# Norm 1 made ahead of its step: statistics two steps earlier, the normalize one step earlier, the transposes of y at the head

## The reference

```python
h = tok(...)                                    # h0, (16, 256, 256)
x = layernorm(h)                                # first norm, then the layer's own norm 1
y = layer_norm(x, norm1_g, norm1_b)
q, k, v = split(y @ qkv_w.T)                    # 16 heads of 16
q, k = elu(q) + 1, elu(k) + 1
att = (q @ (k.T @ v)) / (q @ sum(k) + eps)
x = x + att @ proj_w.T + proj_b
x = x + gelu(layer_norm(x) @ fc1_w.T + fc1_b) @ fc2_w.T + fc2_b
h = h + x
h = h + (leaf_probs(sigmoid(layernorm(h) @ Wq.T @ routers.T)) @ leaf_values) @ Wout_w.T + Wout_b
```

## Time and profile before

| | us |
|---|---|
| median of 3 runs | 540.69 |
| lowest, highest | 537.18, 541.02 |
| profiled execution, its time | 536.7 |
| profiled execution, its span | 534.8 |
| PE busy | 442.4 (83%) |
| VectorE, ScalarE, GpSimd busy | 366.6, 292.2, 193.8 |
| mean granted clock of PE | 0.971 |

### The profile page before, as it was taken

How to read it: one execution, slowest core, us unless ns; L and a number is a source line. 1 busy time by engine, 2 the same in 40 slices (tenths; PEclk the granted TensorE clock), 3 DMA queues, 4 the chain that set the end, 5 groups by cost and what they waited for, 6 DMA issues and landing times.

```text
span 534.8 us, 11443 instructions
## 1 busy us (share of the span) xinstructions
PE 442.4 (83%) x3808; PEld 403.4 (75%) x3808; DVE 366.6 (69%) x867; ACT 292.2 (55%) x604; POOL 193.8 (36%) x187
## 2 busy tenths in 40 slices
PE   0076654988758998799999999999999999998983
PEld 0066654876647888688898898998998998988973
DVE  5999989996657776543747658657567566575674
ACT  3815543757566574465635744754564465366540
POOL 0597996342122212151440620810712514406110
PEclk9997997899899999999999999999999999999997
DMA  4624673425312320010100200201102001001001
GB/s 119 209 86 110 162 202 84 107 83 147 97 53 66 92 96 21 21 39 1 41 2 0 79 0 0 78 0 41 37 0 78 0 0 39 0 0 40 2 16 64
DMA packets 39872, 30.95 MB, mean 58 GB/s; under 512 B 19489, under 2 KB 35233, under 8 KB 39841
## 3 DMA queue, kind: packets, MB, share of 16 engines
q1 hardware_dynamic: 29280, 27.81, 17.2%
q10 hardware_dynamic: 10560, 2.75, 2.3%
HBM read 17.97 MB, written 12.58 MB: 57 GB/s over the span
## 4 chain that ended last, share of the span: by engine, by line
PE 54%; DVE 10%; ACT 3%; issue 3%; POOL 1%; DVEq 0%; POOLq 0%; ACTq 0%
PE PS L307 15%; PE PS L309 15%; PE PS L308 15%; PE PS L1457 5%; PE PS L1568 3%; DVE lTl L1203 1%; DVE xh L1070 1%; PE PS L1466 1%; DVE outb L1263 1%; PE PS L1499 1%; DVE bst L1209 1%; ACT lTh L795 1%; DVE x L1224 0%; DVE fc1l L1169 0%; DVE gl L1232 0%
## 5 line engine op out<-in xcount | busy, mean ns | idle before, releaser
L1232 DVE TENSOR_TENSOR gl<-PS,gh 128x512 fp32r<-128x512 f32 x56 | 38.7, 691 | 62.8 <-ACT gh L803 35.0
L800 ACT ACTIVATE PS<-PS,fc1bias 128x512 f32<-128x512 f32 x56 | 36.7, 655 | 75.3 <-PE PS L309 74.4
L307 PE MATMUL PS<-fc2h,gh 128*128 128x256 f32 x256 | 73.7, 288 | 2.9 <-DVE gl L1232 1.5
L309 PE MATMUL PS<-fc2l,gh 128*128 128x256 f32 x256 | 71.5, 279 | 0.0
L308 PE MATMUL PS<-fc2h,gl 128*128 128x256 f32 x256 | 71.4, 279 | 0.0
L529 POOL TENSOR_SCALAR pst<-mv 128x4 f32<-128x4 f32 x15 | 3.6, 243 | 179.4 <-DVE pst L1216 179.4
L307 PE MATMUL PS<-x2Th,fc1h 128*128 (+2 forms) x144 | 54.6, 379 | 1.5 <-DVE kvm L1108 1.5
L307 PEld LDWEIGHTS PS<-fc2h,gh 128*128 128x128 f32 x256 | 48.0, 188 | 7.0 <-DVE pst L1216 1.6
L308 PE MATMUL PS<-x2Th,fc1l 128*128 (+2 forms) x144 | 53.0, 368 | 0.0
L309 PE MATMUL PS<-x2Tl,fc1h 128*128 (+2 forms) x144 | 52.9, 367 | 0.0
L308 PEld LDWEIGHTS PS<-fc2h,gl 128*128 128x128 f32 x256 | 48.2, 188 | 1.0
(11 more groups left out here) (232 smaller groups left out, 1457.3 us busy)
## 6 DMA issues: line engine op xcount, KB each, us to landing
h<-h_scratch SPq DMA_DIRECT2D x16, 256.0 KB, 3.5
q_scratch<-qe SPq DMA_DIRECT2D x16, 256.0 KB, 2.4
qf<-q_scratch SPq DMA_DIRECT2D x16, 256.0 KB, 3.0
out_tokens<-outb SPq DMA_DIRECT2D x16, 256.0 KB, 2.3
h_scratch<-tokev ACTq DMA_DIRECT2D x10, 256.0 KB, 3.2
craw<-in_c_ri SPq DMA_DIRECT2D x16, 128.0 KB, 2.6
craw<-in_c_ri SPq DMA_DIRECT2D x32, 64.0 KB, 2.4
h_scratch<-tokev SPq DMA_DIRECT2D x6, 256.0 KB, 2.8
```

The costliest lines, as they stand in the source:

```text
L307: pe.matmul(dst, ah, bh, start=start, stop=False, **kw)
L309: return pe.matmul(dst, ah, bl, start=False, stop=stop, **kw)
L800: act.activation(bank(j % 2), bank(j % 2), ACT.Gelu, bias=fc1bias[:, j:j + 1]).then_inc(gact, 1)
L1232: dve.tensor_tensor(gl[:, j % 2, :], bank(j % 2), gh[:, j % 2, :].bitcast(F32), ALU.subtract).then_inc(gldone, 1)
```

## The change

The statistics get a place for each of the 16 steps, so that the wait for the other steps' use goes. stats(s+4) is made in step s while s + 4 < 8, and later by the table STATS (steps 8 and 9 at the end of step 5 and in step 6, two in step 7, then four ahead). xh(s+2) is made in step s, behind y_low(s+1) and q_elu(s) (and, from step 9 on, the mask of the first image), where xh(s+1) stood at the head of the step. T(s+1) goes to the head of step s on PE, before q(s). ScalarE does y_high(s+1) before q_parts(s). GpSimd scales earlier and waits once for xh(0) before it rotates chunk 12. One more load of h0 is issued ahead. In the loop over chunks ScalarE evacuates and stores chunk n before it makes the operands of chunk n+2.

```diff
+STATS = {5: (8,), 6: (9,), 7: (10, 11), 8: (12,), 9: (13,), 10: (14,), 11: (15,)}
...
-        bst1 = sb("bst1", [P, 2, 2, 6])
-        mv1 = sb("mv1", [P, 2, 2, 2])
-        pst1 = sb("pst1", [P, 2, 4, 2])
+        bst1 = sb("bst1", [P, STEPS, 2, 6])
+        mv1 = sb("mv1", [P, STEPS, 2, 2])
+        pst1 = sb("pst1", [P, STEPS, 4, 2])
...
# SyncE
-            load_h0(0)
-            load_h0(1)
-            load_h0(2)
+            for s in range(4):
+                load_h0(s)
...
-                load_h0(n - SINGLE + 2)
+                if n - SINGLE + 3 < GROUPS:
+                    load_h0(n - SINGLE + 3)
...
# GpSimd
-            for n in range(SINGLE, CHUNKS):
-                if n + 1 < CHUNKS:
-                    rotate((n + 1) // 2, (n + 1) % 2)
-                scales(n - FIRST + 2)
+            rotate(SINGLE // 2, 1)
+            scales(0)
+            pool.wait_ge(xh1, CREDIT + 4)
+            rotate(FIRST // 2, 0)
+            scales(1)
+            scales(2)
+            for n in range(FIRST, CHUNKS - 1):
+                rotate((n + 1) // 2, (n + 1) % 2)
+                scales(n - FIRST + 3)
...
# ScalarE, loop over chunks
+            def next_opened(it, par):
+                paired_tables(it + 1, par)
+                closed(it, par)
+                paired_operands(it + 1, par)
+                m_unshifted(it + 1, par)
...
-                    opened(it + 1, par)
-                    closed(it, par)
+                    next_opened(it, par)
...
# ScalarE, chunks 11 to 15, and a step
                 token_row(n - 1)
+                y_high(s + 1)
+                if s >= 0:
+                    q_parts(s)
                 if n + 1 < CHUNKS:
                     operands(n + 1)
-                if s >= 0:
-                    q_parts(s)
-                y_high(s + 1)
-                if n + 1 < CHUNKS:
                     tables(n + 1)
...
             def step(s):
-                q_parts(s)
                 if s + 1 < STEPS:
                     y_high(s + 1)
+                q_parts(s)
                 kv_parts(s, 0)
                 kv_parts(s, 1)
...
# VectorE
+            products(SINGLE, 7)
+            product_sums(SINGLE, SINGLE % 2)
+            norm1_stats(0)
+            one = ones[:, 0:1].unsqueeze(1)
+            link(dve.tensor_copy(vt[:, :, :, P], one.to_broadcast([P, 2, KD])))
+            link(dve.tensor_copy(vt0[:, :, :, P], one.to_broadcast([P, B, KD])))
+            dve.wait_ge(act_set, 1)
+            tt(qkvl[:, :, :], qkvraw[:, :, :], qkvh[:, :, :].bitcast(F32), ALU.subtract)
+            dve.wait_ge(ld_const, 16 * 6)
+            dve.wait_ge(b1copied, 1)
+            tt(fc1bias[:, :], fc1bias[:, :], b1add[:, :], ALU.add)
+            assert count[0] == DVE_ALL
+            norm1_apply(0)
+            norm1_stats(1)
+            products(SINGLE + 1, 7)
+            product_sums(SINGLE + 1, 1)
+            norm1_stats(2)
+            y_low(0)
+            norm1_stats(3)
+            norm1_apply(1)
+            for n in range(FIRST, CHUNKS):
                 s = n - FIRST
-                if s + 1 >= 0:
-                    norm1_apply(s + 1)
                 products(n, 7)
-                if s >= 0:
-                    q_elu(s)
                 product_sums(n, n % 2)
...
+                y_low(s + 1)
+                q_elu(s)
+                norm1_apply(s + 2)
+                if s + 4 < GROUPS:
+                    norm1_stats(s + 4)
+                k_elu(s, 0)
+                k_elu(s, 1)
 
             def step(s):
                 if s + 1 < STEPS:
-                    norm1_apply(s + 1)
+                    y_low(s + 1)
                 q_elu(s)
                 if s > GROUPS:
                     kv_mask(image(s - 1, 0))
-                if s + 1 < STEPS:
-                    y_low(s + 1)
+                if s + 2 < STEPS:
+                    norm1_apply(s + 2)
                 k_elu(s, 0)
-                if s + 2 < STEPS:
-                    norm1_stats(s + 2)
                 if s > GROUPS:
                     kv_mask(image(s - 1, 1))
+                if s > 5:
+                    for x in STATS.get(s, ()):
+                        norm1_stats(x)
                 k_elu(s, 1)
+                if s == 5:
+                    norm1_stats(STATS[5][0])
...
# PE
             def step(s):
+                if s + 1 < STEPS:
+                    y_transposes(s + 1)
                 q_products(s)
                 if s > GROUPS:
                     kv_sums(image(s - 1, 0))
-                if s + 1 < STEPS:
-                    y_transposes(s + 1)
                 kv_products(s, 0)
```

More of the change, by code:

```diff
@@ L490, in scales @@
                 pool.wait_ge(st1, CREDIT + 4 * (s + 1))
-                pool.wait_ge(xh1, CREDIT + 4 * (s - 1))
-                v = mv1[:, s % 2, :, 1]
-                pst = pst1[:, s % 2, :, :]
+                v = mv1[:, s, :, 1]
+                pst = pst1[:, s, :, :]
                 pool.tensor_scalar(pst[:, 0, :], v, EPS, None, ALU.add).then_inc(r1done, 1)
@@ L741, in _ @@
                 for par in range(2):
-                    opened(it + 1, par)
-                    closed(it, par)
+                    next_opened(it, par)
             tables(SINGLE)
+            closed(SINGLE // 2 - 1, 0)
             operands(SINGLE)
-            closed(SINGLE // 2 - 1, 0)
+            closed(SINGLE // 2 - 1, 1)
             operands(SINGLE + 1)
-            closed(SINGLE // 2 - 1, 1)
             tables(SINGLE + 1)
@@ L1056, in norm1_stats @@
                 dve.wait_ge(h0ld[s], 16)
-                dve.wait_ge(xh1, CREDIT + 4 * (s - 1))
                 for i in range(2):
-                    dve.bn_stats(bst1[:, s % 2, i, :], tile(s, i)).then_inc(st1, 1)
+                    dve.bn_stats(bst1[:, s, i, :], tile(s, i)).then_inc(st1, 1)
                 dve.wait_ge(st1, CREDIT + 4 * s + 2)
                 for i in range(2):
-                    dve.bn_aggr(mv1[:, s % 2, i, :], bst1[:, s % 2, i, :]).then_inc(st1, 1)
+                    dve.bn_aggr(mv1[:, s, i, :], bst1[:, s, i, :]).then_inc(st1, 1)
             def norm1_apply(s):
@@ L1069, in norm1_apply @@
                 for i in range(2):
-                    dve.tensor_scalar(xh[:, s % 2 * 2 + i, :], tile(s, i), mv1[:, s % 2, i, 0:1],
-                                      pst1[:, s % 2, 3, i:i + 1], ALU.subtract, ALU.mult).then_inc(xh1, 1)
+                    dve.tensor_scalar(xh[:, s % 2 * 2 + i, :], tile(s, i), mv1[:, s, i, 0:1],
+                                      pst1[:, s, 3, i:i + 1], ALU.subtract, ALU.mult).then_inc(xh1, 1)
                 m, r = (mr[:, x, s // GROUPS, image(s, 0):image(s, 0) + 2] for x in range(2))
-                r1 = pst1[:, s % 2, 2, :]
-                dve.scalar_tensor_tensor(m, mv1[:, s % 2, :, 0], -1.0, r1, ALU.mult, ALU.mult).then_inc(xh1, 1)
+                r1 = pst1[:, s, 2, :]
+                dve.scalar_tensor_tensor(m, mv1[:, s, :, 0], -1.0, r1, ALU.mult, ALU.mult).then_inc(xh1, 1)
                 dve.tensor_copy(r, r1).then_inc(xh1, 1)
@@ L1112, in _ @@
+            for n in range(FIRST, CHUNKS):
                 s = n - FIRST
-                if s + 1 >= 0:
-                    norm1_apply(s + 1)
                 products(n, 7)
-                if s >= 0:
-                    q_elu(s)
                 product_sums(n, n % 2)
-                norm1_stats(s + 2)
[L1120 to L1131, removed]
-                    y_low(s + 1)
-                if s >= 0:
-                    k_elu(s, 0)
-                    k_elu(s, 1)
+                y_low(s + 1)
@@ L1532, in _ @@
                     pe.wait_ge(dve_set, DVE_ALL)
-                if s >= 0:
-                    q_products(s)
                 if s + 1 >= 0:
@@ L1537, in _ @@
                 if s >= 0:
+                    q_products(s)
                     kv_products(s, 0)
```

## The result

The change makes the kernel faster: 519.16 us median (519.01 to 521.34) beside 539.09 (537.18 to 541.02) for the kernel before on the same chip, ratio 0.964 with a 95% interval of 0.9588 to 0.9691. The forecast was 521 in a range of 514.5 to 530; the sum of its terms, 17.0 us off the profiled execution of before (536.7), gave 519.7. The profiled execution of after took 519.01, its span is 517.2.

A forecast was written before the change was run, and what follows sets the result against it. PE was taken to wait 24.6 us for xh and the small operation behind it. Terms 3.8 + 5.3 + 10.7 - 2.8 = 17.0 us off 536.7 gave 519.7; predicted 521, range 514.5 to 530.

The forecast's parts named there:

- Head: Up to T(1), the transposes of step 1: earlier xh brings them at 90.2 us, 3.8 us less.
- Chunk steps: T(1) to T(5): steps of 6.8 us without waits for xh or GpSimd's scale, 5.3 us less.
- rotate: Rival, chunk steps: xh lands on GpSimd's rotate in all four, 9.2 us back, 530 us; chance 0.07.
- Power: Rival, chunk steps: xh waits for the GpSimd scale's power, 3.6 us in all, 525 us; chance 0.10.
- delay of up to 1 us: Chunk steps: one delay of xh by GpSimd's power, taken as absorbed by VectorE's slack.
- Plain steps: T(5) to T(10): 29.1 us in place of 39.8, 10.7 us less.
- The loop over ScalarE: Plain steps: a loop of engines through ScalarE sets each step at 4.95 us, with weight copies paid in full.
- My price of step 8: Plain steps: step 8 waits for VectorE, whose step 7 has two stats; 5.85 us.
- Late steps: T(10) to the end of kv(14,1): late mask stalls the second image's sums 0.7 us a step; 2.8 us more.
- slower: Rival, late steps: the late mask decides; 3.5 us in each of six steps eats all 17; chance 0.04.

The follow-up runs named there:

- e1: The change with xh again one step later and PE and ScalarE in their order of before; 532.52 us, ratio 0.9894 to the kernel before.
- e4: The change without GpSimd's wait for xh(0) before it rotates chunk 12; 521.79 us, ratio 0.9704 to the kernel before.
- e2: The change with the transposes behind q and ScalarE's q_parts before y_high again, xh still early; 537.81 us, ratio 0.9998 to the kernel before.
- e7: The change with one stats to a step from step 5 on; 520.1 us, ratio 0.9662 to the kernel before.
- e3: The change with VectorE's mask of the first image ahead of y_low and q_elu in the late steps; 513.42 us, ratio 0.9553 to the kernel before.
- e5: The change with only ScalarE back in its old order, q_parts before y_high; 545.9 us, ratio 1.0122 to the kernel before.
- e6: e2 with VectorE's mask of the first image ahead of y_low; 518.04 us, ratio 0.9619 to the kernel before.
- e8: e3 plus e7's edit, half of ScalarE's fc2h copy moved behind step 8 and fc1h's halves one step later; 513.06 us, ratio 0.9512 to the kernel before.

## Why the prediction was right, and where it was not

The mechanism that carries the sum, xh made ahead so that PE no longer waits for it, is the one that the runs show: the idle time ahead of T falls from 24.6 to 7.8 us, and with xh late again (e1) most of the gain is gone. The sum was 17.0 us; the spans differ by 17.6. By stage it had 0.4, 0.1 and 0.5 us too much for the head, the chunk and the late steps, and 1.1 and 0.4 too little for the plain steps and the stretch behind. That these cancel is luck; that none is larger is not.

**Head.** T(1) came at 90.57, 0.4 later than worked out. xh(0) was 0.74 us long after 0.89 of idle; the scale's power took 2.41 beside VectorE's weight split of 1.77, and the rest went through as priced. e4 puts 2.2 us of this term on GpSimd's wait for xh. The new order of ScalarE in the loop over chunks, priced at nothing, cost nothing that shows in PE's wait for M: 1.23 us a chunk in after, 1.24 before.

**Chunk steps.** 6.83 a step, in place of 6.8. No xh was held: over all 32 instructions it lasts 0.38 to 0.42 us, so the rival "rotate" did not arise. The mechanism was that the rotate has ended when xh comes, and so it was; what stands under the rotate is the pair of products, which read PSUM and aren't held (GpSimd, then VectorE, in after):

```profile
97.68 1.62 POOL L486 TENSOR_TENSOR Wa<-craw,U 128x768 f32<-128x768 f32 x1 [1.53 <-PE PS L1466]
99.16 1.61 POOL L486 TENSOR_TENSOR Wb<-craw,U 128x768 f32<-128x768 f32 x1
100.85 0.65 POOL L494 TENSOR_SCALAR pst<-mv 128x2 f32<-128x2 f32 x1
```

```profile
96.27 0.73 DVE L1107 SCALAR_TENSOR_TENSOR kvm<-ke,kr 128x256 f32<-128x256 f32 x2
96.91 1.09 DVE L1039 TENSOR_TENSOR PS<-PS,Er 128x896 f32<-128x896 f32 x1
97.91 1.08 DVE L1039 TENSOR_TENSOR Mb<-PS,Ei 128x896 f32<-128x896 f32 x1
```

The prediction looked only at xh. It did not see that k_elu ends 0.7 us before the rotate begins; e2 shows k_elu behind that edge, which costs 2.5 and 2.3 us.

**Power.** The rival is out. In after GpSimd's small sum ahead of the power was itself held (0.65 in place of 0.22), the power came at 101.88, and only the last 0.2 us of xh lay beside it. But e1 has powers over the whole of xh (GpSimd, then VectorE):

```profile
114.78 1.27 POOL L497 TENSOR_TENSOR pst<-pst,halfpow 128x4 f32<-128x4 f32 x1
```

```profile
114.61 0.75 DVE L1108 SCALAR_TENSOR_TENSOR kvm<-ke,kr 128x256 f32<-128x256 f32 x2
115.28 0.73 DVE L1079 TENSOR_SCALAR xh<-h,mv,pst 128x256 f32<-128x256 f32 x2
```

Neither xh nor k_elu was held; it is the power that got longer, 1.27 us in place of 1.03. So the delay of up to 1 us that the prediction took in was none.

**Plain steps.** 28.05 for 29.1 predicted. The loop over ScalarE is there: waits of 1.20, 0.21, 1.69 and 0.90 before T, the long steps (6.03, 6.52) behind the weight copies, no half clock. The five terms of the loop add up to 4.9, not 4.95, which changes the sum by 0.2. The term had the stretch 1.1 us too long: the first step took 4.73, bound by PE, and T(5) to T(9) 22.34 for 23.2. My price of step 8, VectorE with its two stats, was right as a duration (5.85, 5.71), but e7 shows that it isn't worth anything: ScalarE limits steps 8 and 9 together.

**Late steps.** 7.24, 8.30, 7.28, 9.12, 8.24, 7.43 for 7.05, 8.25, 7.2, 9.15, 8.15, 7.35. The stall stands where it was put, ahead of the second sums; the trace names the mask as its end in three of the six and ScalarE's evacuation in step 9 and the last two, but in all six PE starts 0.14 to 0.15 us behind the end of the mask, and moving the mask alone (e3) removes all six. I had it at 0.7 a step and 4.2 in all (the terms that put the mask at 4.8 us after T add up to 4.6, which would have made it 0.5; measured were 0.52 to 0.76, and 1.65 in step 10); taking it away gave 5.7 by the medians (513.42 beside 519.16) and 4.7 by the ratios, and the late stretch is 6.3 shorter. That it was priced somewhat low has its reason in e3: a wait costs 0.24 us beyond its idle time.

**The rival "slower"** had 0.04, and the forecast was right without it. But its mechanism is real and near: e5 is the change without the new order on ScalarE, and it is 1.2% slower than before. I priced the point at which it decides at 3.5 us of stall a step; a stall of 2.3 did it, since the clock falls with it, which added 1.7 a step, and since the plain and chunk steps paid too. The error was to price a stall by its length alone.

**What the gain is made of.** e1 has the head and the statistics: 5.7 us. Adding xh a step ahead alone (e2) shortens the plain steps by another 10.4 (38.8 to 28.4) and lengthens the late ones by 19.5 (43.9 to 63.4, in e2's longest run), which leaves nothing; T at the head with ScalarE's old order (e5) loses 8 more by the medians, 7 by the ratios; the new order on ScalarE turns that into 519. These parts are hard to read one by one, because each of them moves the mask. The runs in which the mask is not late read more plainly. By the ratios to the kernel before, at 539 us: e1, statistics and early xh(0), 5.7 us; e6, xh a step ahead with the mask first, 14.8 more; e3, T at the head with ScalarE's new order, 3.6 more (4.6 by the medians). The change as made is e3 with a late mask, which gives 4.7 back. T's place and ScalarE's order were not separated with the mask first.

## What to carry to other kernels

When work on an in-order engine is moved ahead, follow every instruction that now stands behind it, most of all short ones that read data long ready and that another engine waits for: put these first. Price a stall on PE like the 2.3 us of e2 and e5 with the half clock that may follow (1.7 us more a step there), not by its length. And when one engine closes the loop of a step, what another one saves there is handed to the next step's wait.

## What the runs showed of the hardware

The hold between VectorE and GpSimd depends on the operation. Under a rotate (two operations of 1.6 us, two SBUF inputs each) two k_elu took 3.21 and 3.04 us in place of 0.73 (e2), xh 3.03 in place of 0.74 (e4), the small operation behind it 1.47 in place of 0.15 (e1); each of these instructions ended within 0.2 us of the end of the GpSimd operation that ran. Under the same rotate the products with one PSUM input took 1.08 (after), and the statistics, with one SBUF input, 0.74 (after, 82.69), both as alone. The Trainium skill ("SBUF — State Buffer", "Who interferes with whom", practical consequences) has an instruction hold the shared ports to its end, and names VectorE operations in a 2-port mode or with two SBUF inputs; these rows agree. They also go the other way: GpSimd's sum over two numbers took 0.65 us in place of 0.22 while q_elu, with two SBUF inputs, ran. A GpSimd power (two SBUF inputs of 4 numbers) does not fit: in e1 two k_elu and two xh kept their 0.75 and 0.73 us beside it, and the power itself took 1.27 in place of 1.03. There the measurement decides: not every GpSimd operation that reads SBUF holds VectorE to its end.

TensorE's clock fell to half in every late step of e2 and in most of e5's, behind idle times of 2.3 us some 10 us apart (granted 0.84 and 0.87 over the stretch), and only once in the plain steps of e5, with idle times of 1.8 to 2.0 us some 7 us apart (granted 0.95). In e3 and e8 one and the same idle time of 1.6 us ahead of the gate products gave full clock once and half clock once, and the stretch from the first projection to the end took 323.9 and 325.0 us. So two kernels whose single profiles differ by about 1 us have not been told apart.
